# Whole rows through the scatter: X, mean, deviation, gate and token travel together, and the output is written instead of added to

## The reference, cut to what matters

```python
# x is (32, 64, 128); every block is x = x + block(layernorm(x), ...)
x = x + _L0_xattn_ref(...)      # cross attention, 16 heads
x = x + _L0_ffn_ref(...)        # shared expert + 7 routed, top 2
x = x + _L1_xattn_ref(...)      # two attentions, an LSTM over 64 steps, a feed-forward
# _L1_ffn_ref, tokens = layernorm(x) as (2048, 128):
gates = softmax(tokens @ wg); expert_idx = argmax(gates)
pos = position of the token among those of its expert, in token order
keep = pos < 320                                        # capacity
h = relu(dispatched @ w1 + b1); expert_out = h @ w2 + b2  # per expert, 320 slots
combined = gate * expert_out for kept tokens, 0 for the others
x = x + combined
```

## Time and profile before

| | us |
|---|---|
| median of 3 runs | 740.86 |
| lowest, highest | 739.43, 752.29 |
| the profiled execution, own time | 741.43 |
| its span | 739.5 |
| its mean granted TensorE clock | 0.974 of full |

### The profile page before, as it was taken

The page is one execution under the profiler, slowest core; times in us unless marked ns, Lnnn a source line. Parts: engine busy times, 40 slices in busy tenths (PEclk is TensorE's granted clock), DMA queues, the critical chain, the costliest instruction groups (busy, mean ns, idle before and its releaser), DMA issues.

```text
span 739.5 us, 16640 instructions
## 1 busy us (share of the span) xinstructions
PE 671.3 (91%) x6559; PEld 569.3 (77%) x6559; DVE 439.0 (59%) x1152; ACT 344.0 (47%) x930; POOL 133.2 (18%) x220
## 2 busy tenths in 40 slices
PE   1799999999999999989999998999999999796992
PEld 0477778988889888867676676899999999543772
DVE  5499857748746657679899998233343444410221
ACT  0489852333222222357788786355554544101331
POOL 4425740010000000024000010000000000062576
PEclk9999999999999999989999999999999999788997
DMA  7500300000000000123322100000000000213222
GB/s 258 171 18 20 132 3 1 1 1 1 1 1 1 1 0 1 48 66 77 83 66 67 36 7 2 1 2 2 1 2 2 1 1 2 58 40 90 18 21 20
DMA packets 30006, 24.46 MB, mean 33 GB/s; under 512 B 3825, under 2 KB 27122, under 8 KB 29554
## 3 DMA queue, kind: packets, MB, share of 16 engines
q1 hardware_dynamic: 26482, 21.40, 10.0%
q0 software_dynamic: 3456, 2.12, 2.1%
HBM read 17.96 MB, written 5.80 MB: 32 GB/s over the span
## 4 chain that ended last, share of the span: by engine, by line
PE 78%; DVE 11%; issue 5%; ACT 2%; POOL 2%; DMA 1%; POOLq 0%; DVEq 0%; SPq 0%; ACTq 0%
PE SC L665 15%; PE PT L675 12%; PE MI L594 5%; PE SC L844 5%; PE PT L584 5%; PE SC L575 3%; PE SC L933 3%; PE SC L765 3%; PE SC L804 2%; PE PJ L551 2%; DVE kexp L1216 2%; PE SC L768 2%; PE SC L809 2%; PE SC L771 2%; PE PT L815 2%
## 5 line engine op out<-in xcount | busy, mean ns | idle before, releaser
L1048 ACT ACTIVATE big<-SC 128x512 f32<-128x512 f32 x88 | 52.6, 599 | 144.3 <-PE SC L665 144.3
L675 PEld LDWEIGHTS PT<-wd,big 128*128 128x128 f32 (+1 forms) x768 | 90.2, 191 | 2.5 <-issue 0.4
L675 PE MATMUL PT<-wd,big 128*128 128x128 f32 (+1 forms) x768 | 90.6, 274 | 0.0
L1378 DVE TENSOR_TENSOR big<-SC,big 128x512 f32<-128x512 f32 (+1 forms) x88 | 60.5, 689 | 41.7 <-PE SC L665 32.4
L665 PE MATMUL SC<-xP,wgP 128*128 128x512 f32 x264 | 78.8, 407 | 0.7 <-DVE big L1378 0.3
L665 PE MATMUL SC<-xP,wuP 128*128 128x512 f32 x264 | 74.4, 390 | 0.0
L594 PEld LDWEIGHTS MI<-vblk,PTs 128*64 128x64 f32 x1536 | 50.1, 140 | 11.7 <-ACT oT L998 2.8
L594 PE MATMUL MI<-vblk,PTs 128*64 128x18 f32 x1536 | 54.5, 214 | 4.7 <-ACT big L1003 1.7
L665 PEld LDWEIGHTS SC<-xP,wuP 128*128 128x128 f32 x264 | 49.6, 188 | 10.9
L993 ACT ACTIVATE PTs<-PT 128x512 f32<-128x512 f32 x96 | 52.3, 595 | 6.6 <-PE PT L584 5.5
L584 PE MATMUL PT<-ident,sc 128*128 128x128 f32 x384 | 53.6, 284 | 0.6 <-ACT sc L988 0.6
(11 more groups left out here) (223 smaller groups left out, 1331.5 us busy)
## 6 DMA issues: line engine op xcount, KB each, us to landing
kvs<-in_ctxT SPq DMA_DIRECT2D x32, 64.0 KB, 1.9
w1s<-in_e1w SPq DMA_DIRECT2D x8, 256.0 KB, 2.8
w2s<-in_e1w SPq DMA_DIRECT2D x8, 256.0 KB, 3.3
wg<-in_wg SPq DMA_DIRECT2D x1, 1408.0 KB, 8.9
wu<-in_wu SPq DMA_DIRECT2D x1, 1408.0 KB, 11.9
slots_in<-big SPq DMA_DIRECT2D x1, 1300.0 KB, 6.0
big<-slots_in SPq DMA_DIRECT2D x8, 130.0 KB, 2.4
wd<-in_wd SPq DMA_DIRECT2D x2, 512.0 KB, 13.9
```

The source lines that it names most:

```text
L675: last = pe.matmul(PT[:, e % 2, t * P:t * P + P], h[0:w, t * P:t * P + P], wd[0:w, e, c, :], start=(c == 0), stop=(c == 2))
L1048: act.activation(sg[a % 2], SC[:, a % 2, :], ACT.Silu).then_inc(s["silu_done"], 1)
L1378: last = dve.tensor_tensor(hT[e % 2][0:w, c, :], SC[0:w, 2 + a % 2, :], sg[a % 2][0:w, :], ALU.mult)
```

## The change

- `DR` goes from 130 to 132. A new buffer `XR` holds rows of X, mean, reciprocal deviation, gate and token number, and the scatter sends its rows. `XN` keeps 128 columns and feeds the gate's logits only. SP copies each tile of X into `XR` when the LSTM's feed-forward has been added to it, 16 DMAs from SBUF to SBUF; POOL copies mean, deviation and token for all tiles in three instructions.
- Behind the load VectorE normalises each expert's rows into `xnE` (`normed`, three instructions), and the transposes wait for this instead of for the load. It is done two experts ahead, except for experts 0 and 1.
- The output row is made whole on VectorE: X + gate * bias while the products run, and + gate * product from the bank behind them. `y_scale` on ScalarE is gone. POOL's three indirect DMAs per expert write the rows, no longer accumulating.
- `BURST` goes from 20 to 28.
- Second attention: `pv` of step 1 stands ahead of `proj`. The four late transposes go one each into steps 8 to 11 and into free columns of PJ, with one ScalarE copy of 128 columns each in steps 9 to 12.
- LSTM: the gate products of block 1 go from steps 0, 0, 1, 2 to steps 1, 1, 2, 2; step 0 has two more warming matmuls instead.

```diff
-DR = D + 2
+DR = D + 4
-BURST = 20
+BURST = 28
-LAST_ROWS = 9
+LAST_ROWS = 8
-        XN = big[:, 4096:4096 + NT * DR].rearrange("p (i d) -> p i d", i=NT)
+        XR = big[:, 2048:2048 + NT * DR].rearrange("p (i d) -> p i d", i=NT)
+        XN = big[:, 4160:4160 + NT * D].rearrange("p (i d) -> p i d", i=NT)
...
+        xnE = [spent[:, (7 + 3 * i) * P:(10 + 3 * i) * P].rearrange("p (c d) -> p c d", c=3) for i in range(2)]
...
-            sp.wait_ge(s["f_added"], NT)
+            for i in range(NT):
+                sp.wait_ge(s["f_added"], i + 1)
+                sp.dma_start(XR[:, i, 0:D], X[:, i, :]).then_inc(s["row_kept"], 16)
...
-            pool.tensor_copy(XN[:, :, D + 1:D + 2], token[:, :].unsqueeze(2)).then_inc(s["token_kept"], 1)
+            pool.wait_ge(s["ln_xn"], 3 * GRP + len(GROUPS))
+            pool.tensor_copy(XR[:, :, D:D + 1], mean[:, :].unsqueeze(2))
+            pool.tensor_copy(XR[:, :, D + 1:D + 2], rstd[:, :].unsqueeze(2))
+            pool.tensor_copy(XR[:, :, D + 3:D + 4], token[:, :].unsqueeze(2)).then_inc(s["token_kept"], 1)
...
+            pool.wait_ge(s["row_kept"], 16 * NT)
...
-                                        XN[:, i, :], None, bounds_check=NSLOT - 1, oob_is_err=False
+                                        XR[:, i, :], None, bounds_check=NSLOT - 1, oob_is_err=False
...
-                                            yo[p][0:w, c, :], None, bounds_check=T - 1, oob_is_err=False,
-                                            compute_op=ALU.add).then_inc(y_added[p], 16)
+                                            yo[p][0:w, c, :], None, bounds_check=T - 1, oob_is_err=False
+                                            ).then_inc(y_added[p], 16)
...
+                if known(m, 1):
+                    pv(n - 1, 1 - p, (v - 1) % 4)
+                if isinstance(m, int) and 0 <= m - LAST_ROWS < 4:
+                    pe.wait_ge(s["kexp_ready"], n + 3)
+                    pe.wait_ge(s["ln_xn"], 3 * GRP)
+                    pe.transpose(PJ[:, 384:512], xn_last[:, m - LAST_ROWS, :], ident[:, :])
                 if not known(m, NU1 - 3, NU1 - 2, NU1 - 1):
                     proj(2 - p, n + 3, i + 1 + p, 1 - p)
-                if known(m, LAST_ROWS):
-                    pe.wait_ge(s["ot_copied"], n - 1)
-                    rows_turned(3 * GRP - 1, MI)
+                if known(m, LAST_ROWS + 5):
                     pe.wait_ge(s["ln_evacuated"], 3 * GRP)
-                if not known(m, 0):
+                if not known(m, 0, 1):
...
-                if t == 0:
-                    gate_in(1, 0)
-                if j < BLK - 1 and more > 0:
+                if t in (1, 2):
+                    gate_in(1, 2 * t - 2)
+                    gate_in(1, 2 * t - 1)
+                elif t == 0:
+                    keep_warm(PT[:, 0, :], 2)
+                elif j < BLK - 1 and more > 0:
                     gate_in(k + 1, j + 1)
...
-                pe.wait_ge(xin_loaded[e], 32)
+                pe.wait_ge(s["xin_normed"], e + 1)
...
-                    last = pe.transpose(PT[:, p, o:o + w], xin[e][0:w, c, 0:D], ident[0:w, 0:w])
+                    last = pe.transpose(PT[:, p, o:o + w], xnE[p][0:w, c, :], ident[0:w, 0:w])
...
-                wait(pe, s["y_biased"], e - 1)
+                wait(pe, s["y_ready"], e - 1)
...
+                if isinstance(m, int) and 0 <= m - LAST_ROWS - 1 < 4:
+                    o = (11 + m - LAST_ROWS) * P
+                    act.wait_ge(s["proj_done"], n + 3)
+                    last = act.activation(xnT[:, o:o + P], PJ[:, 384:512], ACT.Copy)
...
-                if known(m, LAST_ROWS):
-                    rows_kept(3 * GRP - 1, MI)
...
-                if e:
-                    y_scale(e - 1, (e - 1) % 2)
-            y_scale(E1 - 1, (E1 - 1) % 2)
...
+            def normed(e, p):
+                dve.wait_ge(xin_loaded[e], 32)
+                wait(dve, s["xin_transposed"], e - 1)
+                for c, (_, w) in enumerate(SL):
+                    last = dve.tensor_scalar(xnE[p][0:w, c, :], xin[e][0:w, c, 0:D], xin[e][0:w, c, D:D + 1],
+                                             xin[e][0:w, c, D + 1:D + 2], ALU.subtract, ALU.mult)
+                last.then_inc(s["xin_normed"], 1)
+
             def expert(e, p):
-                dve.wait_ge(xin_loaded[e], 32)
...
+                wait(dve, y_added[p], 48 * (e // 2))
+                for c, (_, w) in enumerate(SL):
+                    last = dve.scalar_tensor_tensor(yo[p][0:w, c, :], b2r[0:w, e, :], xin[e][0:w, c, D + 2:D + 3],
+                                                    xin[e][0:w, c, 0:D], ALU.mult, ALU.add)
+                last.then_inc(s["y_biased"], 1)
+                if e < E1 - 2:
+                    normed(e + 2, p)
+                dve.wait_ge(s["y_biased"], e + 1)
                 dve.wait_ge(s["e2_done"], e + 1)
-
-                wait(dve, y_added[p], 48 * (e // 2))
-                bias = b2r[:, bass.ds(e, 1), :]
-                dve.tensor_tensor(yo[p][:, 0:2, :], TPB[p][:, 0:2 * P].rearrange("p (c d) -> p c d", c=2),
-                                  bias.broadcast_to([P, 2, D]), ALU.add)
-                dve.tensor_tensor(yo[p][0:64, 2:3, :], TPB[p][0:64, 2 * P:3 * P].unsqueeze(1), bias[0:64, :, :],
-                                  ALU.add).then_inc(s["y_biased"], 1)
+                for c, (_, w) in enumerate(SL):
+                    last = dve.scalar_tensor_tensor(yo[p][0:w, c, :], TPB[p][0:w, c * P:c * P + P],
+                                                    xin[e][0:w, c, D + 2:D + 3], yo[p][0:w, c, :], ALU.mult, ALU.add)
+                last.then_inc(s["y_ready"], 1)
             dve.wait_ge(s["b2r_loaded"], 80)
+            normed(0, 0)
+            normed(1, 1)
```

More of the change, by code:

```diff
@@ L233, in build @@
             gates_done o_gate_done first_tanh tanh_done o_done ab_done c_done tc_done h_ready
-            f_done relu_done f2_done f_added rows_transposed rows_evacuated last_evacuated rows_logits rows_copied token_kept
+            f_done relu_done f2_done f_added rows_transposed rows_evacuated last_evacuated rows_logits rows_copied token_kept row_kept
             gate_step gexp_ready onehot_ready hot_turned hot_copied sums_done sums_copied count_done slots_ready scattered pool_newton
-            xin_transposed xin_copied e1_done e1_relu_a e1_relu_v e2_done y_biased y_ready
+            xin_normed xin_transposed xin_copied e1_done e1_relu_a e1_relu_v e2_done y_biased y_ready
             out_stored""".split()
@@ L523, in rows_turned @@
                 pe.wait_ge(s["ln_xn"], m + 1)
-                rows_of = xn_last if m == 3 * GRP - 1 else xn[m % 2]
                 for t in range(4):
-                    last = pe.transpose(bank[:, t * P:t * P + P], rows_of[:, t, :], ident[:, :])
+                    last = pe.transpose(bank[:, t * P:t * P + P], xn[m % 2][:, t, :], ident[:, :])
                 last.then_inc(s["ln_transposed"], 1)
@@ L1067, in step1 @@
                 n, p = NU0 + m, v % 2
+                if isinstance(m, int) and 0 <= m - LAST_ROWS - 1 < 4:
+                    o = (11 + m - LAST_ROWS) * P
+                    act.wait_ge(s["proj_done"], n + 3)
+                    last = act.activation(xnT[:, o:o + P], PJ[:, 384:512], ACT.Copy)
+                    if m == LAST_ROWS + 4:
+                        last.then_inc(s["ln_evacuated"], 1)
                 if not known(m, NU1 - 2, NU1 - 1):
@@ L1112, in lstm_pair @@
                         act.activation(tc[u][:, :], c2[u][:, :], ACT.Tanh, scale=0.5).then_inc(s["tc_done"], 1)
-                        if t == 0:
-                            g_copy(1, 1, 0)
-                        if j < BLK - 1 and more - kp > 0:
+                        if t in (1, 2):
+                            g_copy(1, 1, 2 * t - 2)
+                            g_copy(1, 1, 2 * t - 1)
+                        elif 0 < t and j < BLK - 1 and more - kp > 0:
                             g_copy(k + 1, 1 - kp, j + 1)
@@ L1143, in expert @@
                     xin_copy(e + 1, 1 - p)
-            def y_scale(e, p):
-                act.wait_ge(s["y_biased"], e + 1)
-                for c, (_, w) in enumerate(SL):
-                    last = act.activation(yo[p][0:w, c, :], yo[p][0:w, c, :], ACT.Copy, scale=xin[e][0:w, c, D:D + 1])
-                last.then_inc(s["y_ready"], 1)
             xin_copy(0, 0)
@@ L1542, in _ @@
             link(dve.tensor_reduce(v1[:, :], r1[:, :, :], AX.X, ALU.max))
-            link(dve.tensor_tensor(XN[:, :, D:D + 1], v1[:, :].unsqueeze(2), v3[:, :].unsqueeze(2), ALU.mult))
+            link(dve.tensor_tensor(XR[:, :, D + 2:D + 3], v1[:, :].unsqueeze(2), v3[:, :].unsqueeze(2), ALU.mult))
             dve.wait_ge(s["count_done"], 1)
@@ L1549, in _ @@
             dve.tensor_scalar(slot[:, :], v4[:, :], NOWHERE, None, ALU.add).then_inc(s["slots_ready"], 1)
+            def normed(e, p):
[5 more added lines that the diff above has]
+                last.then_inc(s["xin_normed"], 1)
```

(5 more changed lines are left out.)

## The result

The changed kernel takes 738.31 us (median of 20 runs, 735.05 to 740.81), the kernel before 742.86 (median of 20 runs beside it, 739.04 to 752.68). The ratio is 0.9932, with an interval of 0.9916 to 0.9949: 3.8 to 6.2 us less, about 5. That is within the 2% that one measurement here tells from no change, but twenty runs on each side settle its sign. The forecast was 7.9 us less and 733.0 us.

What follows compares the result with a forecast made beforehand. TensorE was taken to pace the experts and VectorE the second attention. Terms of -1.3 - 4.2 - 2.4 - 0.9 + 0.9 = -7.9 us took the median 740.86 to 733.0 us, range about 729.5 to 739.

Steps and rivals of the forecast that it cites:

- the experts' start: Ahead of the first expert: normalising and clock, +0.9 - 2.2 = -1.3 us, with the larger burst ending before the transposes.
- steps 1 and 2: Second attention: moving `pv` into the wait for `kexp` removes VectorE's waits, -2.4 us, bounds 0 and -2.9.
- steps 8 to 12: Second attention: spreading four late transposes over four steps gives -0.9 us, bounds -1.2 and +0.2.
- the prediction's own signs of being wrong: Experts over 6.1 us apart, no idle before VectorE's first ReLU, or burst still running when normalised rows are there.
- The experts' end: From the last matmul to the kernel's end: 8.1 us against 12.3, so -4.2 us.
- stays at the adding price: Rival: the output's plain DMAs cost as much as accumulating ones, 2.1 us dearer, 735.1 us; chance 0.15.
- the burst overruns: Rival at the first expert: the warming burst ends late or the clock is low anyway, up to 735.2 us; chance 0.13.
- The experts' middle: Between experts: VectorE's added instructions fit with 0.2 us to spare, cost 0; experts stay 6.08 us apart.
- the slower rival: At the experts, VectorE stops POOL while it writes descriptors; at the adding price about 751 us; chance 0.03.
- the rival's 2.4 us: Rival: the second attention's early gain does not come, as ScalarE's or VectorE's order ends the waits, 735.4 us; chance 0.13.
- LSTM: Steps 0 to 3, reordered gate products: -1.55 in step 0, twice +1.2 after, sum +0.9 us, bounds -1.5 and +1.4.

Runs made afterwards that it cites:

- c0_changed: The changed kernel run again unaltered, as a control: 737.55 us, ratio 0.9895 to the kernel before.
- d2_plain_out: The kernel before with only the accumulation left out of the output's indirect DMAs: 740.51 us, ratio 0.9964.
- c3_old_gates: The changed kernel with the old order of the LSTM's gate products: 734.67 us, ratio 0.9868.
- d1_attention: The kernel before with only the two edits of the second attention: 739.94 us, ratio 0.996.
- d4_new_gates: The kernel before with only the new order of the gate products: 743.75 us, ratio 1.0012.
- c1_burst24: The changed kernel with 4 x 24 warming matmuls instead of 4 x 28: 738.1 us, ratio 0.992.
- c2: The changed kernel with the old burst of 4 x 20 warming matmuls: 737.8 us, ratio 0.9914.
- e2_two_banks: The changed kernel with the second block's gate products on two banks, in steps 0, 1, 1, 2: 736.11 us, ratio 0.9883.
- e4: The changed kernel with the old order of the gate products, repeated on another chip: 736.57 us, ratio 0.9884.
- d3_burst28: The kernel before with only the longer burst, 4 x 28 warming matmuls: 746.86 us, ratio 1.0038.
- e1_warm_attention: The changed kernel with the old gate order and matmuls in TensorE's idle places at the second attention's start: 736.63 us, ratio 0.9897.
- e3_all_three: The changed kernel with gate products on two banks, filler matmuls at the second attention's start and a 4 x 26 burst: 732.61 us, ratio 0.9829.

## Why the prediction was right, and where it was not

**Direction, range and the likeliest time.** The time lies in the range (729.5 to 739.0) and within 2% of before, as foretold, but 5 us above the likeliest 733.0. Two of these are the run of before itself: its median was 740.86 over three runs and 742.86 over twenty. The other 3 are terms of the sum, as worked out below: 1.2 at the experts' start, 0.7 at their end, 1.6 in steps 1 and 2, less 0.3 in steps 8 to 12. The range held them because it was wide, and one of the prediction's own signs of being wrong came: the burst was still running when the normalised rows were there.

**The experts' end: right in mechanism, 0.7 short.** G went from 12.32 to 8.79, -3.5 for -4.2. VectorE's three instructions took 0.86 (said 0.9), POOL began 727.27 - 726.48 = 0.8 behind (0.9), the two further starts took 2.56 (2.5). The row of the scatter was the right price for the instruction, 0.972. The mis-sized term is what follows the last start: 734.3 - 729.83 = 4.5 for the 3.8 of landing and end. Before, it was 739.5 - 734.52 = 5.0. So landing gave back 0.5, where the scatter's 2.3 for 3.2 would have given 0.9. The reason is that the last DMA is the one of 64 rows, and the sum took the figures of 128: by itself it landed 2.5 us after issue before, and 2.0 in c0_changed, which leaves 2.5 for the end of the program in both (4.98 - 2.5, and 735.4 - 730.9 - 2.0), not 1.5. The Trainium skill (DMA: Bandwidth & Descriptors, Anatomy of one DMA) would have had it give back nothing; the measurement lies between. Experiment d2_plain_out splits the 3.5: 2.8 by the plain write, 0.7 by the new order of bias and scaling. The rival "stays at the adding price" fell.

**The experts' start: this step failed.** The sum had +0.9 for the normalising and -2.2 for the clock. Both came: the transposes can start 1.0 us behind the load (D less the load in c0_changed: 26.51 - 25.51), and E fell from 4.92 to 3.16. What failed is "by this 32 more end it at about 675.7, still before 676.0". That left 0.3 us, from rows that held no idle time; even without any, the burst of c0_changed ended 26.6 us behind the slots, where the sum had 25.85. In six executions with 4 x 28 behind the changed load, F was 78.12, 76.46, 76.30, 78.59, 77.55 and 78.41, a mean of 77.57; in the four with the old start and 4 x 20 (before, d1_attention, d2_plain_out, d4_new_gates) 77.33, 77.12, 78.09 and 78.22, a mean of 77.69. So the term is -0.1, not -1.3. When the burst ends in time (c0_changed and c3_old_gates, mean 76.38) it is the -1.3 of the sum. The rival "the burst overruns" had 0.13 and came true in four of six, in which the transposes came 1.4 to 2.4 us behind the normalised rows. Both its price and its chance were too low: it put the overrun at 0.9 us (676.9 for 676.0), and in the profiled execution it was 675.58 - 673.47 = 2.1.

**The experts' middle: right.** 6.08 us apart before and after; VectorE had 0.21 to 0.29 us idle ahead of its first ReLU, as the 0.2 of the sum, at six of seven places. At the fourth (702.57) it had none, since its additions began 0.35 us later there, in five other traces too; what delays them the rows don't name, and the ReLU still began on time. POOL's DMA instructions had a maximum of 1.010 us, though VectorE works with two SBUF operands beside them (L1581 at 722.28 beside the DMA at 722.47): at most 0.04 us over the median is all that it costs, and the slower rival fell. (In d2_plain_out, without these instructions of VectorE, the maximum was 0.978.) The Trainium skill (SBUF — State Buffer, SBUF: two separate sides) has a VectorE instruction with two SBUF inputs block a GpSimd one only if that reads SBUF; the prediction left this condition out. No DMA instruction of this trace was shut out.

**Attention, steps 1 and 2: right size, wrong certainty.** The profiled execution has the forecast's picture: the wait of 1.43 ahead of the projection is 0.39, and A fell by 2.7 (said 2.4, with 2.9 where the clock stays up):

```profile
323.56 0.46 PE L558 MATMUL PJ<-xnT,wat 128*128 128x128 f32 x2 [0.39 <-DVE kexp L1227]
```

But the step took the clock's fall at 325 for a property of the place. Over the eight executions with the moved `pv` and nothing in the idle places (changed, c0, c1, c2, c3, d1, e2, e4), A was 7.9 three times and 11.1 five times, a mean of 9.9; over the four without the move (before, d2, d3, d4) it was 10.4 to 11.4, a mean of 10.7. That is -0.8 on the mean. But the clock fell at one of two places (worked out from the mean clock of stretches of 2 us): 0.5 to 0.9 us behind the first bias addition (five of the eight, and d3_burst28 of the four), or 5.0 to 5.3 us behind it, in the wait (the other three of the four, none of the eight). With the early fall A is 11.1 with the move and 11.36 without; without it 7.9 and 10.5. So the edit is worth -0.2 or -2.6, by whether the clock has fallen ahead of it. As the early fall stands ahead of the moved `pv`, its five in eight against one in four may be chance; were it as frequent on both sides (six of twelve), the mean would be -1.4 (estimate). That the waits go back to TensorE was right; the rival's 2.4 us were mostly lost, by a mechanism that it didn't name.

**Attention, steps 8 to 12: right.** B went from 9.93 to 8.74, -1.2 for -0.9. The 0.3 for two transposes on the binding chain wasn't paid.

**LSTM: right.** +0.91 for +0.9. Step by step it came a little otherwise: the first hidden states are 3.21, 3.61 and 3.62 us apart, where before they were 4.91, 2.31 and 2.31, so step 0 gave 1.7 (said 1.55) and the two others cost 1.3 each (said 1.2). The wait for the copy was the larger part of a second product's 1.3, as e2_two_banks showed, and its own work the rest.

**The sum anew.** -0.1 start, -3.5 end, -0.8 and -1.2 attention, +0.9 LSTM: -4.7, against 4.6 between the medians and 5.0 by the ratio. The parts come from few executions each, so that the agreement is partly luck: with -1.4 for steps 1 and 2 it would be -5.3.

## What the runs showed of the hardware that I had not expected

The granted clock is a part of the time that differs from run to run. In 63 runs of the kernel before on these chips the time went from 739.05 us, with a mean clock of 0.974, to 753.75 us, with 0.950; the 13 with 0.974 all lie between 739.05 and 741.64, the 6 with 0.952 or less between 747.83 and 753.75. Where a fall sits in the trace it costs 3 to 4.4 us: A of 11.1 for 7.9, 13.3 for 8.9 in steps 5 to 7. The falls near 320 and 325 come behind some microseconds in which TensorE has several pieces of idle time, none over 1.5 us, and not each time: about 320 or about 325, or not at all, in the same code. The fall of d4_new_gates at about 342 has no such pieces in the 10 us ahead of it, so idle time just before is not the whole cause; what is, no run here shows.

A loop of identical matmuls that wait for nothing can stand idle. In five of seven profiled bursts of 4 x 28 (changed, d3_burst28, e1, e2 and e4), and in the 4 x 26 of e3_all_three, TensorE paused 0.7 to 1.8 us in all, some 22 us behind the burst's start, at "issue"; the bursts of c0_changed and c3_old_gates ran through, and so did the 4 x 24 of c1_burst24, 23 us long. With e1_warm_attention as the longest:

```profile
671.00 5.12 PE L567 MATMUL SC<-warm 128*128 128x512 bf16 x22 [1.75 <-issue]
```

It is no matter of the iteration (22 us lie in another place of a loop of 26 than of 28) and in the changed kernel it begins 0.6 us behind the end of POOL's last scatter instruction; what makes it wasn't tested.

## What to carry to other kernels

A burst that bridges a wait should be sized by its longest execution, not by the mean of one: here 0.3 us of margin were lost to 1.6 us of idle time that the rows didn't hold, too short a burst cost as much through the clock, and 4 x 26 in the one execution seen kept clear of both. When a gain hangs on the granted clock of one stretch, look at several executions before giving it its full price. And two products that share one bank with a copy between cost the next step 1.3 us; through two banks the second one cost 0.6, so that moving products between steps pays only by what each step can hide.
